# Wavelet, convolution and median kernel: an earlier wait on GpSimd, earlier seeds, and three images summed by TensorE and put out by ACT

## What is computed

```python
cA, cH, cV, cD = dwt2(x)                      # Haar bands, 16 x 16 each
proc = lambda c: batchnorm_relu(einsum('bchw,oc->bohw', c, conv_w), bn_gamma, bn_beta)
rimg0 = idwt2(proc(cA), proc(cH), proc(cV), proc(cD))
rimg1 = idwt2(...)                            # three levels forth and back: x again
y = conv3x3(concatenate([rimg0, rimg1], axis=1), convW_w) + convW_b
y = batchnorm_relu(y, bnW_gamma, bnW_beta)    # statistics over all images: the second norm
med = median_blur(y, 3)                       # 3 x 3 median, zero padded
out = y + einsum('bchw,oc->bohw', med, W) + b
```

## Time and profile before

| | |
|---|---|
| median of 3 runs | 421.12 us (420.78 to 421.69) |
| profiled execution, its own time | 423.23 us |
| span of its instructions | 421.3 us |
| TensorE busy | 397.0 us, 94% |
| VectorE busy | 383.4 us, 91% |
| GpSimd, ACT busy | 194.5 us (46%), 152.8 us (36%) |
| mean granted TensorE clock | 0.987 of full |

### The profile page before, as it was taken

One profiled execution on the slowest core, in us unless ns is written; L12 is line 12 of the kernel. 1 busy time (PEld: TensorE's weight loads), 2 busy tenths in 40 slices (PEclk: granted clock), 3 DMA queues, 4 the chain that ended last, 5 costly groups with the idle time before them and its releaser, 6 DMA issues.

```text
span 421.3 us, 3650 instructions
## 1 busy us (share of the span) xinstructions
PE 397.0 (94%) x1119; PEld 210.2 (50%) x1120; DVE 383.4 (91%) x532; ACT 152.8 (36%) x348; POOL 194.5 (46%) x194
## 2 busy tenths in 40 slices
PE   7889999999999999999999999999999967997875
PEld 2335588846444444444444444444455856862331
DVE  3899857999849999999999999999999999999974
ACT  2465763412262423324141414232233211249820
POOL 3999395713443552637344444536272700006700
PEclk9999999999999999999999999999999996999989
DMA  7970200100101101010110101010100000002656
GB/s 280 418 322 3 96 4 2 50 0 2 51 0 50 51 0 51 0 50 0 51 50 1 50 0 52 0 50 1 50 0 2 0 1 2 0 0 100 249 205 246
DMA packets 7796, 26.72 MB, mean 63 GB/s; under 512 B 992, under 2 KB 1248, under 8 KB 7776
## 3 DMA queue, kind: packets, MB, share of 16 engines
q1 hardware_dynamic: 7776, 26.48, 16.6%
HBM read 18.09 MB, written 8.39 MB: 63 GB/s over the span
## 4 chain that ended last, share of the span: by engine, by line
PE 62%; DVE 21%; POOL 7%; issue 7%; DMA 2%; ACT 1%; SPq 0%; POOLq 0%; DVEq 0%
PE conv_ps L381 55%; DVE y L914 3%; PE one_ps L363 3%; PE one_ps L446 2%; PE conv_ps L469 2%; POOL y L212 2%; POOL y L213 2%; DMA ru<-x 2%; DVE one_ps L842 1%; DVE sorted_cols L838 1%; DVE sorted_cols L794 1%; DVE sorted_cols L834 1%; DVE sorted_cols L790 1%; DVE z L823 1%; DVE one_ps L821 1%
## 5 line engine op out<-in xcount | busy, mean ns | idle before, releaser
L381 PE MATMUL conv_ps<-ru,wt 128*128 128x512 f32 (+1 forms) x360 | 132.4, 504 | 0.0
L381 PEld LDWEIGHTS conv_ps<-ru,wt 128*128 128x128 f32 x360 | 69.1, 192 | 53.6 <-issue 50.1
L381 PE MATMUL conv_ps<-xu,wt 128*128 128x496 f32 (+3 forms) x240 | 89.2, 509 | 6.2 <-DVE conv_ps L757 6.2
L569 ACT ACTIVATE y<-conv_ps,sgn 128x512 f32<-128x512 f32 (+1 forms) x40 | 25.5, 637 | 170.8 <-PE conv_ps L381 170.8
L381 PEld LDWEIGHTS conv_ps<-xu,wt 128*128 128x128 f32 x240 | 46.7, 195 | 42.3 <-issue 33.2
L219 POOL TENSOR_TENSOR ru<-z 128x512 f32<-128x512 f32 x14 | 17.9, 1276 | 83.7 <-DVE one_ps L827 83.2
L381 PE MATMUL conv_ps<-ru,v 128*128 128x496 f32 (+3 forms) x120 | 43.9, 501 | 0.3 <-POOL ru L220 0.3
L381 PE MATMUL conv_ps<-y,v 128*128 128x496 f32 (+3 forms) x108 | 38.6, 491 | 0.0
L381 PE MATMUL conv_ps<-y,wt 128*128 128x496 f32 (+3 forms) x108 | 38.6, 491 | 0.0
L469 PE MATMUL conv_ps<-z,w 128*128 128x512 f32 x64 | 31.8, 640 | 6.0 <-DVE y L914 6.0
L318 POOL TENSOR_TENSOR ru<-eo 128x512 f32<-128x512 f32 x16 | 17.0, 1060 | 43.3 <-PE conv_ps L381 42.8
(11 more groups left out here) (128 smaller groups left out, 646.6 us busy)
## 6 DMA issues: line engine op xcount, KB each, us to landing
raw<-x SPq DMA_DIRECT2D x20, 512.0 KB, 3.3
out<-y SPq DMA_DIRECT2D x15, 512.0 KB, 2.6
ru<-x SPq DMA_DIRECT2D x8, 512.0 KB, 9.0
xu<-x SPq DMA_DIRECT2D x4, 512.0 KB, 9.0
wt<-w_t SPq DMA_DIRECT2D x2, 576.0 KB, 10.7
out<-y SPq DMA_DIRECT2D x2, 256.0 KB, 3.2
w<-w_t SPq DMA_DIRECT2D x2, 64.0 KB, 4.6
vec<-vectors SPq DMA_DIRECT2D x1, 3.0 KB, 9.7
```

Source lines behind the costliest of these rows:

```text
L381: return nc.tensor.matmul(bank(u, b)[:, (r0 - row) * BW:(r1 - row) * BW], taps(half, kx, ky), plane[:, (r0 + dy) * BW:(r1 + dy) * BW], sta ...
L569: S.activation(at(slot(n), row * W + b, [[2, cols]]), src, ACT.Identity, scale=sgn[:, :], accum_out=y_sum[:, part:part + 1]).then_inc(y_ke ...
```

## The change

- GpSimd: `make_ru03(n)` waits for rows_read of image n-2 in place of y_done of image n-2; the rows_read wait ahead of `make_xu03(n)` is gone.
- Medians of images 12 and 13 write their seeds early.
- A unit matrix is made on GpSimd. For images 3, 7 and 11 (`SUMMED`), ACT writes relu(norm(y)) in place, TensorE adds it onto the mix by two calls with the unit matrix, and ACT reads the sum from PSUM, adds b and writes the image. ACT's finish of image n comes behind its norm of median n+2. VectorE finishes the other 13 images (`OWN`), eleven of them before the end of image 15's median (the new `FINISH_AT`).
- ACT maps x1 of image 15 as before; GpSimd's maps are unchanged.

```diff
-    BN3_AT, FINISH_AT = 8, (17, 18, 20, 21, 22, 24, 25, 27, 28)
+    BN3_AT, FINISH_AT = 8, (15, 16, 17, 19, 20, 21, 23, 24, 25, 27, 28)
+    SUMMED = (3, 7, 11)
+    OWN = [n for n in range(IMAGES) if n not in SUMMED]
...
                 if n < 2:
                     wait_xu12(pool, 2 + RING + n)
                 else:
-                    pool.wait_ge(y_done, 2 * (last_unit(n - 2) + 1))
+                    pool.wait_ge(rows_read, last_unit(n - 2) + 1)
...
                 make_ru03(n)
-                pool.wait_ge(rows_read, last_unit(n - 2) + 1)
                 make_xu03(n)
+            G.memset(unit[:, :], 1.0).then_inc(ones_set, 1)
+            pool.wait_ge(ones_set, 1)
+            G.affine_select(out=unit[:, :], in_=unit[:, :], pattern=[[-1, CH]], base=0, channel_multiplier=1,
+                            compare_op=ALU.is_equal, fill=0.0).then_inc(unit_made, 1)
...
+                    half = slice(b * BANK, (b + 1) * BANK)
+                    mm = nc.tensor.matmul(conv_ps[:, k, half], w2[:, :], zslot(n)[:, half], start=True, stop=n in OWN)
+                    if n in SUMMED:
+                        pe.wait_ge(x1_by_act, n // 4 + 1)
+                        mm = nc.tensor.matmul(conv_ps[:, k, half], unit[:, :], slot(n)[:, half], start=False, stop=True)
...
             for n in range(2, IMAGES):
-                pe.wait_ge(out_ready, n - 1)
+                if n - 2 in SUMMED:
+                    pe.wait_ge(out_by_act, SUMMED.index(n - 2) + 1)
+                else:
+                    pe.wait_ge(out_ready, OWN.index(n - 2) + 1)
                 mix(n, n % 2)
...
+            for n in range(1, IMAGES):
                 norm_median(n)
+                if n in SUMMED:
+                    S.activation(slot(n), slot(n), ACT.Relu, bias=shift3[:, :], scale=scale3[:, :]).then_inc(x1_by_act, 1)
+                if n - 2 in SUMMED:
+                    act.wait_ge(mix_done, n - 1)
+                    S.activation(slot(n - 2), conv_ps[:, n % 2, :], ACT.Identity, bias=cb2).then_inc(out_by_act, 1)
...
-                early, late = (seeds, None) if n in HALVED else (None, seeds)
+                early, late = (seeds, None) if n in HALVED or n + 2 in HALVED else (None, seeds)
...
-            for n in range(len(FINISH_AT), IMAGES - 1):
+            for n in OWN[len(FINISH_AT):-1]:
                 finish(n)
```

More of the change, by code:

```diff
@@ L93, in wavelet_conv_median_kernel @@
         w2 = sb("w2", [CH, CH])
+        unit = sb("unit", [CH, CH])
         p_kept = [sb(f"p_kept{k}", [CH, BANK]) for k in range(2)]
@@ L183, in wavelet_conv_median_kernel @@
         mix_done = sem("mix_done")
+        ones_set = sem("ones_set")
+        unit_made = sem("unit_made")
+        out_by_act = sem("out_by_act")
         out_ready = sem("out_ready")
@@ L249, in _ @@
             for n in range(IMAGES - 1):
-                sp.wait_ge(out_ready, n + 1)
+                if n in SUMMED:
+                    sp.wait_ge(out_by_act, SUMMED.index(n) + 1)
+                else:
+                    sp.wait_ge(out_ready, OWN.index(n) + 1)
                 sp.dma_start(out_img[:, n, :], slot(n)).then_inc(out_sent, 16)
             for part in range(2):
-                sp.wait_ge(out_ready, IMAGES + part)
+                sp.wait_ge(out_ready, len(OWN) + part)
                 half = slice(part * HALF, (part + 1) * HALF)
@@ L468, in mix @@
                         pe.wait_ge(half_ready, b + 1)
-                    mm = nc.tensor.matmul(conv_ps[:, k, b * BANK:(b + 1) * BANK], w2[:, :], zslot(n)[:, b * BANK:(b + 1) * BANK],
-                                          start=True, stop=True)
+                    half = slice(b * BANK, (b + 1) * BANK)
[3 more added lines that the diff above has]
+                        mm = nc.tensor.matmul(conv_ps[:, k, half], unit[:, :], slot(n)[:, half], start=False, stop=True)
                     if b == 1 or n == IMAGES - 1:
@@ L478, in _ @@
             pe.wait_ge(w2_in, 16)
+            pe.wait_ge(unit_made, 1)
             pe.wait_ge(squares_summed, PARTS_ALL)
@@ L618, in norm_median @@
                 S.activation(zslot(n), zslot(n), ACT.Relu, bias=shift3[:, :], scale=scale3[:, :]).then_inc(med_normed, 1)
-            def map_x1(n):
-                S.activation(slot(n), slot(n), ACT.Identity, bias=shift3_bias2[:, :], scale=scale3[:, :]).then_inc(x1_by_act, 1)
-            for n in range(1, 4):
+            for n in range(1, IMAGES):
                 norm_median(n)
[L625 to L630, removed]
+                if n in SUMMED:
+                    S.activation(slot(n), slot(n), ACT.Relu, bias=shift3[:, :], scale=scale3[:, :]).then_inc(x1_by_act, 1)
+                if n - 2 in SUMMED:
+                    act.wait_ge(mix_done, n - 1)
+                    S.activation(slot(n - 2), conv_ps[:, n % 2, :], ACT.Identity, bias=cb2).then_inc(out_by_act, 1)
+            last = slot(IMAGES - 1)
+            S.activation(last, last, ACT.Identity, bias=shift3_bias2[:, :], scale=scale3[:, :]).then_inc(x1_by_act, 1)
         @block.vector
@@ L916, in _ @@
             place = {BN3_AT: second_batch_norm}
-            for n, instruction in enumerate(FINISH_AT):
+            for n, instruction in zip(OWN, FINISH_AT):
                 place[instruction] = lambda n=n: finish(n)
```

## The result

The changed kernel takes 423.71 us (421.65 to 424.60, 16 executions) against 421.43 us (16 executions) of the kernel before: a ratio of 1.0038, 95% interval 1.0021 to 1.0056, so some 1.6 us (0.9 to 2.4) **slower**. A second comparison gave 423.69 against 422.05 us, ratio 1.0026 (1.0007 to 1.0045). The profiled execution took 423.88 us with a span of 421.9 us.

The account below looks back on a forecast made before the run. TensorE bounds until 313 us, VectorE through the last four medians, then TensorE again. Last finish 418.5 plus transfer 3.5 gives 422.0 against span 421.3, +0.6; added to 421.12 this makes 421.7 us, range 419.4 to 423.4.

Parts of the forecast that it names:

- within 0.2%: Whole kernel: outcome "same", within 0.2% (0.84 us) of the time before; chance 0.40, against faster 0.24 and slower 0.36.
- Part 1: GpSimd's ru03 waits for rows_read instead of y_done: 0.5 us on TensorE plus 1.04 on VectorE, 1.54 us gained.
- Part 2: Early seeds, medians 12 and 13: VectorE loses 0.5 us, half clock 1.7 to 2.8; second norm at 374.5, 0.5 earlier.
- Unit matrix: GpSimd's memset and affine_select at some 337 us, perhaps beside VectorE's L817: 0.1 us, bounds 0 to 1.0.
- The tail's chain: Mixes 2 to 12 at 1.71 us per image hold up VectorE's finishes; last median ends 412.8, last finish 418.5.
- Last transfer: After the last finish: stands less behind other transfers than before, taken as 3.5 us in place of 3.7.
- The difference carries over: From span to median: profiled 422.0 against a span of 421.3, +0.6 us, added to median 421.12 gives 421.7.
- Seam between calls: Rival, tail: each met wait between TensorE calls costs 0.10 us, 1.7 us in place of 0.3: 423.1; chance 0.15.
- Clock before the norm: Rival: outputs(15a) and (15b) at half clock, loss over 2.8 us, norm 0.5 us or more late: 422.7; chance 0.17.
- Clock kept at mix(15): Rival, tail: TensorE keeps full clock at mix(15), saving 1.4 us: 420.3; chance 0.16.
- TensorE doesn't bind: Rival, tail: doubled mixes are hidden and VectorE runs through, median end 406: 413.5, half of that 418; chance 0.08.
- enough for half clock: Tail: 2.1 us of TensorE idling before 405.87 brought half clock, so 4.3 us before mix(15) would too, costing 1.4 us.

Follow-up runs that it names:

- a_warm_mix15: Changed kernel plus 18 matmuls on zeros on TensorE between mix(14) and mix(15): 421.63 us, ratio 0.9980 to the kernel before.
- a_fin8: Changed kernel with eight VectorE finishes ahead of the last median's end in place of eleven, every instruction kept: 417.96 us, ratio 0.9908 to the kernel before.
- a_again: Changed kernel run once more, nothing edited: ratio 1.0026 to the kernel before, span 422.1 us.
- a_no_unit_calls: Changed kernel without the unit-matrix matmuls, waits and ACT's finishes kept: 418.84 us, ratio 0.9929 to the kernel before.
- p12_wait_seeds: Kernel before with GpSimd's moved wait and early seeds for medians 12 and 13, without the tail's change: 421.70 us, ratio 0.9975.
- a_warm_conv: Changed kernel plus 16 matmuls on zeros in TensorE's wait before outputs(15b): 422.45 us, ratio 1.0015 to the kernel before.

## Why the prediction was right, and where it wasn't

Put on the 421.12 us that the forecast started from, the ratio of 1.0038 gives 422.7 us, inside the range of 419.4 to 423.4; the median itself, 423.71, lies 0.3 above it. The worked-out time (a little slower) had the direction right, but not the size: 0.6 us were forecast, 1.1 to 1.6 measured, and "within 0.2%" had the largest of the three chances.

- **Part 1, 1.54 us.** Right in both terms: no TensorE wait at 154 us (the step starts at 154.09, 2.52 behind the one of 151.57), L805 at 0.69. Alone it measured 1.6 us.
- **Part 2.** Waits of 2.2 and 5.1 us were forecast; they are 2.30 and 4.97. Outputs(15b) starts at 366.38; 0.42 of the 0.48 us by which that is late come from the load stage. The half clock costs 2.6 us (375.35 - 366.38 - 6.4), inside the 1.7 to 2.8 but above the 2.2 taken. So the **norm was mis-sized**: 375.35 in place of 374.5, inside its bounds; 0.42 of it is the load stage, the rest mostly the clock. The forecast's own terms (norm 1.54 us earlier by part 1, 0.5 with part 2) make part 2 a loss of 1.0 us, which it never set apart; the profiles have 1.5 us at the norm, the times 0.5 us (old tail) and 1.4 to 1.9 us (new tail).
- **Unit matrix, 0.1 us.** The affine_select took 0.29 us at 337.72 and L837 beside it 0.66 to the next start in place of 0.60: 0.06. The Trainium skill, SBUF — State Buffer, section SBUF: two separate sides, says that the later of two such instructions waits out the earlier one; these overlap by 0.18 us at 337.83, and less than that was lost, so that the trace doesn't bear the rule out here; spans on GpSimd are rough, though.
- **The tail's chain.** From the norm to finish(12) 32.3 us were forecast, and 32.31 measured. Finish waits of 2.2, 2.9, 2.3 came as 2.18, 2.86, 2.20; median end 412.8 as 413.64; mix(15) 414.3 as 415.31; last finish 418.5 as 419.49. All of it is the norm's 0.85 us carried along, and 0.1 to 0.2: mix(15) comes 1.67 us behind the median's end, where 1.4 were put (and 412.8 + 1.4 is 414.2, not 414.3). The loss by half clock at mix(15), 1.4 us, is 4.18 - 2.75 = 1.43.
- **Last transfer: mis-sized.** 3.5 us were taken, 2.4 measured. Of the two halves' transfers (the page's DMA rows, before and then after):

```profile
out<-y SPq DMA_DIRECT2D x2, 256.0 KB, 3.2
```

```profile
out<-y SPq DMA_DIRECT2D x2, 256.0 KB, 2.1
```

The last numbers are us from issue to landing. Windows of 417 to 418 us, before and then after (the last three columns are clock, DMA share and GB/s):

```profile
417.00:418.00 1.00, 0.00 (x0) 0.00 (x0) 0.64 (x1) 0.00 (x0) 0.00 (x0) 1.00 1.01 410
```

```profile
417.00:418.00 1.00, 1.00 (x2) 0.06 (x1) 0.75 (x1) 0.00 (x0) 0.00 (x0) 0.50 0.02 4
```

Before, image 14 is finished at 416.1 us and still on its way (a whole image lands 2.6 us after its issue, by the page) when the first half of image 15 is issued at 416.8. After, it is finished at 414.9 and out by 417 us; the DMA engines are idle (0.02) until the first half goes at 417.8, and the second follows 1.7 us later. The idle engines seem to be the larger part: in a_warm_mix15 the halves lie 0.86 us apart as before, and land after 2.3 us; in a_fin8, with image 14 close ahead, after 3.1. The forecast had the reason right and took 0.2 us for it. These 1.1 us made up for the norm, and the span (422.0 forecast, 421.9 measured) came out right by luck: two errors cancel.
- **From the span to the median: the step that failed.** "The difference carries over" took the profiled execution of after to stand as far above its median as that of before (423.23) did. Before's stood 1.8 above its median (421.43), after's 0.2 above its own (423.71). (The difference of the spans is rounded: 422.0 less 421.3 is 0.7, where the sum has 0.6.) The executions of both kernels spread over some 3 us (before 420.59 to 423.80, after 421.65 to 424.60). What puts one low or high isn't settled; two things of that size are in the traces, the load stage (41.3 to 42.8 us) and the pattern of the clock ahead of the norm (0.8 us, below).

The rivals. Seam between calls: fallen; two unit calls and two mix calls lie 0.43 us apart, and a late release costs 0.1 to 0.2 us, where 0.10 was taken. Clock before the norm: the loss of 2.6 us stays short of its 2.8; the norm is 0.35 us later than before, and 0.42 of that is the load stage. Clock kept at mix(15): fallen, and the run that forces it gives the 1.4 us. "TensorE doesn't bind": fallen as to its reason, yet its time (413.5 to 418) is where a_fin8 lies, by TensorE binding without a gap. The forecast treated `FINISH_AT` as given, and never priced it by itself; it moves the time by 5 us or more, where 0.6 were forecast for the whole change.

## What to carry to other kernels

When a helper engine takes work off the bound engine, follow the chain that the work is moved into: here 5.1 us of matmuls were added, and the engine that was meant to be relieved waits 7.2 us for its inputs ahead of the last median's end. An instruction that waits in an in-order queue delays everything behind it; before changing who does the work, look for the places in the queue where each consumer's input is already there (5.0 to 5.7 us here, with no instruction changed). And a difference of two profiled executions is only as good as where each stands in its own kernel's spread.

## What the runs showed of the hardware

**One gap, two patterns of the clock.** After the same 2.30 us wait ahead of 15a the clock stayed full in five of the profiled executions that have it (after, a_again, a_no_unit_calls, p12_wait_seeds, a_warm_conv) and fell in two, a_fin8 and a_warm_mix15. TensorE's instructions up to that point are the same in all seven. Windows of a_fin8:

```profile
356.00:359.00 3.00, 3.00 (x9) 2.45 (x8) 2.93 (x7) 0.13 (x1) 0.00 (x0) 0.53 0.00 0
359.00:361.00 2.00, 2.00 (x9) 1.73 (x8) 2.00 (x4) 0.98 (x4) 0.00 (x0) 0.85 0.00 0
366.00:370.00 4.00, 4.00 (x13) 3.26 (x12) 3.93 (x8) 0.76 (x3) 0.00 (x0) 0.57 0.00 0
407.00:410.00 3.00, 3.00 (x8) 1.37 (x8) 2.13 (x3) 1.48 (x2) 0.60 (x2) 1.00 0.63 257
```

It runs at half clock from 356.2 to about 359.6 and again from 366.4 to about 369.8, where after has one stretch of 6.8 us (364.5 to 371.4). The first one is partly hidden: outputs(15a) ends later and the wait ahead of 15b is 3.28 us rather than 4.97. The norm comes 0.7 to 1.0 us earlier than with the long stretch. Nothing in these kernels was found that sets the pattern, and part 2's cost at the norm follows it (0.8 us in these two profiles, 1.5 to 1.8 in the others). The Trainium skill, TensorE: Matmul & The Clock Gate, section Part 1: The HAM clock gate (the "warmup" mystery), says of the start of a kernel that the number of slow matmuls differs from run to run. These traces show the like in mid kernel.

The tail has the same case. Before mix 11 TensorE waits 2.13 us in before and in p12_wait_seeds, and the twenty records behind it take 10.55 us with a stretch at half clock and, in p12_wait_seeds, 8.85 us at full clock:

```profile
406.15 8.85 PE L468 MATMUL conv_ps<-z,w 128*128 128x512 f32 x20 [2.13 <-DVE y L913]
```

So a wait of 2.1 to 2.3 us may or may not cost the clock, 1.7 us in this case, and a forecast should carry both. The prediction read the one row of before as a rule ("enough for half clock"); for its own gap, 4.3 us, each of the five traces that have it shows half clock in mix 15 (3.05 to 3.75 us from its start to its end, in place of 1.98).

**ACT reading PSUM isn't slower.** ACT's finish, 1024 fp32 columns of PSUM, takes 1.11 to 1.12 us; its norm of 1024 columns from SBUF takes 1.23 to 1.24.

**A memset and an affine_select of 128x128 fp32 on GpSimd** take 0.21 and 0.29 us.
